# First layer's queries as seven half products per pair of heads, with keys and values of all heads computed first

## What is computed

```python
q = (query @ Wq).reshape(b, t, h, d)      # query = layernorm(x), b 16, t 64, h 32 heads, d 128
k = (key @ Wk).reshape(b, t, kv_h, d)     # key = value = context, 8 key/value heads
v = (value @ Wv).reshape(b, t, kv_h, d)
q = apply_rope(q)                         # x*cos + rotate_half(x)*sin
k = apply_rope(k)
logits = einsum('btkgd,bTkd->bkgtT', q, k) * ATTN_MULT
logits = 30 * tanh(logits / 30)
logits = where(mask, logits, -1e30)
attn = einsum('bkgtT,bTkd->btkgd', softmax(logits), v)
x = x + attn.reshape(b, t, h * d) @ Wo
```

## Time and profile before

| | before |
|---|---|
| median of 3 runs | 831.82 us (831.56 to 831.97) |
| profiled execution, its span | 830.6 us |
| TensorE busy | 825.8 us, 99% |
| VectorE busy | 549.1 us, 66% |
| ScalarE busy | 369.7 us, 45% |
| GpSimd busy | 361.4 us, 44% |
| granted TensorE clock | full speed in all 40 slices |

### The profile page before, as it was taken

The page is one execution under the profiler, slowest core; times in us unless marked ns, Lnnn a source line. Parts: engine busy times, 40 slices in busy tenths (PEclk is TensorE's granted clock), DMA queues, the critical chain, the costliest instruction groups (busy, mean ns, idle before and its releaser), DMA issues.

```text
span 830.6 us, 11973 instructions
## 1 busy us (share of the span) xinstructions
PE 825.8 (99%) x4382; PEld 687.4 (83%) x4382; DVE 549.1 (66%) x1091; ACT 369.7 (45%) x920; POOL 361.4 (44%) x279
## 2 busy tenths in 40 slices
PE   9999999999999999999999999999999999999998
PEld 7888888877887877877877788898988888888887
DVE  6866956767776564747767746464366657677894
ACT  6443223124213123122223142567797877777762
POOL 4777444545638324443645340112232432356442
PEclk9999999999999999999999999999999999999999
DMA  8122311311403202110311313011010210300002
GB/s 310 52 64 69 85 52 40 101 52 52 124 16 103 64 1 73 43 52 13 103 51 37 94 50 84 14 38 51 14 39 26 54 25 24 128 14 1 2 1 102
DMA packets 25786, 48.12 MB, mean 58 GB/s; under 512 B 4608, under 2 KB 5888, under 8 KB 25600
## 3 DMA queue, kind: packets, MB, share of 16 engines
q1 hardware_dynamic: 25296, 46.70, 19.0%
q10 hardware_dynamic: 432, 0.66, 0.2%
HBM read 45.12 MB, written 2.23 MB: 57 GB/s over the span
## 4 chain that ended last, share of the span: by engine, by line
PE 98%; DMA 1%; DVE 0%; ACT 0%; issue 0%; ACTq 0%; DVEq 0%
PE PB L1411 23%; PE PB L1412 23%; PE PB L1413 23%; PE PB L1627 8%; PE PB L1558 4%; PE PB L1541 4%; PE PB L1418 3%; PE PB L1642 3%; PE PB L1455 2%; PE PB L1453 2%; PE PB L1450 2%; DMA arena<-in_ctxT 1%; PE PB L1579 1%; PE PB L1593 0%; PE PB L1480 0%; PE PB L1473 0%
## 5 line engine op out<-in xcount | busy, mean ns | idle before, releaser
L912 POOL TENSOR_TENSOR qb<-qb,arena 128x512 f32<-128x512 f32 x64 | 83.8, 1310 | 151.1 <-DVE arena L1256 151.1
L1167 DVE TENSOR_TENSOR xs<-xs,PB 128x512 f32<-128x512 f32 x111 | 75.5, 686 | 79.0 <-PE PB L1413 70.0
L989 ACT ACTIVATE Oh<-PB 96x128 fp32r<-96x128 f32 (+2 forms) x236 | 79.4, 360 | 66.4 <-PE PB L1558 47.3
L1411 PE MATMUL PB<-WOh,Oh 128*128 128x512 f32 x242 | 94.5, 390 | 0.0
L1413 PE MATMUL PB<-WOh,Ol 128*128 128x512 f32 x242 | 94.2, 389 | 0.0
L1412 PE MATMUL PB<-WOl,Oh 128*128 128x512 f32 x242 | 94.2, 389 | 0.0
L989 ACT ACTIVATE WOh<-stage 128x512 fp32r<-128x512 f32 (+1 forms) x32 | 19.2, 620 | 132.6 <-PE PB L1413 132.6
L889 POOL TENSOR_TENSOR WOl<-stage,WOh 128x512 fp32r<-128x512 f32 (+1 forms) x32 | 40.7, 1284 | 83.5 <-ACT WOh L989 63.6
L889 POOL TENSOR_TENSOR WQl<-stage,WQh 128x512 fp32r<-128x512 f32 x38 | 49.0, 1293 | 61.7 <-ACT WQh L989 52.1
L1411 PE MATMUL PB<-xTh,WQh 128*128 128x512 f32 x188 | 74.8, 398 | 0.0
L1412 PE MATMUL PB<-xTl,WQh 128*128 128x512 f32 x188 | 73.3, 390 | 0.0
(11 more groups left out here) (294 smaller groups left out, 2171.2 us busy)
## 6 DMA issues: line engine op xcount, KB each, us to landing
stage<-in_wq SPq DMA_DIRECT2D x44, 256.0 KB, 2.7
stage<-in_wo SPq DMA_DIRECT2D x44, 256.0 KB, 2.7
arena<-recs SPq DMA_DIRECT2D x32, 256.0 KB, 3.9
stage<-in_wk SPq DMA_DIRECT2D x12, 256.0 KB, 2.6
xs<-in_x SPq DMA_DIRECT2D x8, 256.0 KB, 7.3
out<-xs SPq DMA_DIRECT2D x7, 256.0 KB, 2.0
arena<-in_ctxT SPq DMA_DIRECT2D x6, 256.0 KB, 7.0
stage<-in_wv SPq DMA_DIRECT2D x4, 256.0 KB, 4.8
```

The lines of the kernel that those rows point to most:

```text
L912: e.tensor_tensor(dst, dst, tmp, ALU.add).then_inc(s_radd)
L989: return e.activation(dst, src, ACT.Copy)
L1167: e.tensor_tensor(xs[:, i, :], xs[:, i, :], PB[b][:, :], ALU.add).then_inc(free[b])
L1411: e.matmul(dst, Ah, Bh, start=(k == 0), stop=False)
```

## The change

Per pair of query heads that belong to one key/value head (the pair is two of the group's four heads; u counts 14 pairs, of key/value heads 1 to 7) the four blocks of its queries (two heads, two halves of the tokens) are computed by Winograd's form of the product of two 2x2 block matrices: seven block products instead of eight, each of an inner dimension of 256 (two blocks of 128, so 6 matmuls). The factors of three of them are blocks as they are or two of them (products 1, 2, 3), of the others sums of blocks:

- x: the two halves of the tokens by the two halves of the inner dimension are the blocks. They are kept in f32 as `xf` when x is turned; four sums of them are formed once (`xt`, VectorE) and split to Th, Tl (`xt_split`: ScalarE, then VectorE or GpSimd), in the place of the context's parts.
- weights: `split wp u 0` and `wp u 1` split the two heads' weights into a buffer WS (1792 columns: head one whole, of head two the second block, then the four sums); GpSimd forms the four sums in `wsum` from the staged f32 weights (VectorE for u < 2), ScalarE writes their high part and GpSimd their low part (`pair`, 1024 columns each).
- products: 1, 6, 7, 4 accumulate one upon the other in one bank, 5 and 3 in a second, 2 alone in a third. ScalarE copies the bank after products 1, 5 and 6 into `held` (`snap`), VectorE adds products 2, 3 and 7 to these copies (`cmb`); the four finished tiles are the held ones and product 4's bank.
- rotations of these tiles (`rope p u t`, `sin u t`): ScalarE writes the two swapped, negated halves into a buffer rtmp, VectorE multiplies by cos into qb (a separate operation on the held tile, SBUF, for t < 3) and the buffer by sin in place (SBUF), GpSimd adds.

The queries of key/value head 0 (`q0`) stay as they were. Keys and values of all heads come first, in a stage before the loop: keys of heads 2 to 7 and values of heads 4 to 7 are written to DRAM (`keys`, `vals`; twenty spills of 256 KB on SyncE's queue out of eight slots in qb) and read back when a buffer comes free (`k_in`, `v_in`). The context's split parts go to DRAM (`ctx_out`, 4 MB in two DMAs) and come back at the end of the loop for layer 1 (`ctx_in`, issued by ScalarE). Homes of several split weights move, and `weff_load` is placed six turns earlier in layer 1's loop, behind a later wait.

In the loop's turn u a product pair stands for the four query steps, in pieces between the output tiles; the splits of the next pair's weights, `pair`, and in odd turns four splits of output weights are placed as the diff shows.

```diff
@@ plan @@
+    def more(self, *name, of):
+        bank, uses, _ = self.banks[of]
+        self.filled[bank] += 1
+        self.banks[name] = (bank, uses, self.filled[bank])
+        self.step(*name)
...
+    def products(u, *ks):
+        for k in ks:
+            if k in (6, 7, 4):
+                p.more("p", u, k, of=("p", u, 1))
+            elif k == 3:
+                p.more("p", u, k, of=("p", u, 5))
+            else:
+                stage("p", u, k, bank={1: 4 if u == 1 else 5, 2: 7, 5: 0}[k])
+            if k in (1, 5, 6):
+                step("snap", u, k)
+            elif k != 4:
+                step("cmb", u, k)
+
     for u in range(NU):
...
+        if u < 3:
+            products(u, 1, 2)
+            query(0)
+        burst(u)
+        if u % 2 and u <= 11:
+            step("k_in", (u + 3) // 2)
+        if u in (5, 9):
+            step("v_in", (u - 5) // 4)
+        query(3)
+        if u in (1, *range(3, NU)):
+            norm0(u - 1)
...
+        if quad:
+            if u >= 3:
+                products(u, 1, 2)
+            products(u, 5)
+            rope_p(u, 0)
+            sin(u, 0)
+        if u not in (1, 2):
+            step("sum0", u)
+            step("sum0_out", u)
+        outputs(0)
...
+        if quad:
+            products(u, 6, 3)
+            rope_p(u, 1)
+        if 0 < u < NU - 3:
+            for n in range(2):
+                split("wp", u + 1, n)
+        outputs(1)
+        if quad:
+            products(u, 7)
+            sin(u, 1)
+            query(2)
+            rope_p(u, 2)
+            sin(u, 2)
+        if u == 2:
+            norm0(1)
+        if u in (1, 2):
+            step("sum0", u)
+            step("sum0_out", u)
+        outputs(2)
+        if quad:
+            products(u, 4)
+            rope_p(u, 3)
+            sin(u, 3)
+        if 0 < u < NU - 3:
+            step("pair", u + 1)
+        outputs(3)
+        if u % 2:
+            for n in range(4):
+                split("wo0", 2 * u - 2 + n)
@@ gpsimd_program @@
+                            e.tensor_tensor(parts[0], other[:, 0:256], other[:, 256:512], ALU.add).then_inc(s_ws)
+                            e.tensor_tensor(parts[2], src[:, 0:256], other[:, 0:256], ALU.subtract).then_inc(s_ws)
+                            pool.wait_ge(s_ws, 4 * u + 1)
+                            e.tensor_tensor(parts[1], parts[0], src[:, 0:256], ALU.subtract).then_inc(s_ws)
+                            pool.wait_ge(s_ws, 4 * u + 3)
+                            e.tensor_tensor(parts[3], src[:, 256:512], parts[1], ALU.subtract).then_inc(s_ws)
...
+                elif kind == "pair" and k[0] >= 2:
+                    u, = k
+                    hi, lo = WS[1 - u % 2]
+                    pool.wait_ge(s_wshi, u + 1)
+                    e.tensor_tensor(lo[:, 768:1792], wsum[:, :], hi[:, 768:1792].bitcast(f32), ALU.subtract).then_inc(s_wslo)
@@ scalar_program @@
+                elif kind == "snap":
+                    u, t = k
+                    act.wait_ge(*done("p", u, t))
+                    if u:
+                        act.wait_ge(s_sin, 4 * u - {1: 3, 6: 2, 5: 1}[t])
+                    move(held[t], PB[bank_of("p", u, t)][:, :]).then_inc(s_snap)
+                elif kind == "rope" and k[0] == "p":
...
+                    act.wait_ge(s_radd, n - 2)
+                    for r in range(2):
+                        last = e.activation(tmp_of(n)[64 * r:64 * r + 64], src[64 - 64 * r:128 - 64 * r], ACT.Copy, scale=-1.0)
+                    last.then_inc(s_swap)
@@ vector_program @@
+                elif kind == "rope" and k[0] == "p":
...
+                    cos = e.tensor_tensor(dst, src.rearrange("p (b t) -> p b t", b=8), ropeq[:, 0:1, :].broadcast_to([128, 8, 64]), ALU.mult)
...
+                elif kind == "sin":
...
+                    e.tensor_tensor(tmp, tmp, ropeq[:, 1:2, :].broadcast_to([128, 8, 64]), ALU.mult).then_inc(s_sin)
+                elif kind == "cmb":
...
+                    e.tensor_tensor(kept, PB[bank_of("p", u, t)][:, :], kept, ALU.add).then_inc(s_cmb)
@@ tensor_program @@
+                    pe.wait_ge(*(lo_ready("wp", u, t // 4) if t in (1, 2, 4) else (s_wslo, u + 1)))
...
+                    fresh = t in (1, 2, 5)
+                    for c in range(2):
+                        w = slice(c0 + 128 * c, c0 + 128 * c + 128)
+                        for n, (W, X) in enumerate(((Wh, Xh), (Wh, Xl), (Wl, Xh))):
+                            last = e.matmul(PB[b][:, :], W[:, w], X[:, c, :], start=fresh and c == n == 0, stop=(c == 1 and n == 2),
+                                            skip_group_check=not fresh)
+                    last.then_inc(full[b])
```

534 lines of the change are left out of this document (412 added, 122 removed).

## The result

| | before | after |
|---|---|---|
| median of 4 runs | 831.69 us | 885.79 us (885.31 to 886.53) |
| profiled execution, its span | 830.6 us | 883.8 us |
| TensorE busy | 99% | 94% |
| two units in the middle of the loop | 57.0 us (scores at 198.70 and 255.72), TensorE full, products of later keys and values among them | 55.6 us, of which TensorE's work needs 48.4 |

The ratio is 1.0646, 95% interval 1.0631 to 1.0661: 54.1 us slower. The forecast was 858 us, range 824 to 872; the direction was right, the size half of what was measured.

A forecast was written before the change was run, and what follows sets the result against it. The prediction took TensorE, busy 99% of the span and holding 98% of the chain, to bound the kernel. From 831.8 us, -19.0 (products), +32 (loop) and +13 (opening) gave 858 us, range 824 to 872.

The forecast's parts named there:

- The products saved: TensorE's query products: 84 fewer at 0.226 us each, -19.0 us.
- The new first stage: Keys and values of all heads ahead of the queries: same products, 0 to +4 us, taken as 0.
- The loop: Units 2 to 13: waits through the other engines' queues outlast TensorE's work; 7 to 35 us, taken as +32.
- The eleven steps: Loop from one unit's mask to the next without TensorE: 21.8 us, 22.4 with handoffs; 55 for two units with turns.
- step 5: In the loop, ScalarE's high part of the next pair's weights, behind its swap for the second rotation: 0.6 us.
- the port's turns: VectorE operations with two SBUF inputs alternate with GpSimd's: up to 0.55 us each; two units 55 us against 51.5.
- B: Rival: the loop without most turns and an opening of 8; 836 us, 829 to 843, chance 0.19.
- C: Rival: a loop link seen wrongly, two units take TensorE's 48.4, opening costs 5; 818 us, 813 to 824, chance 0.17.
- The opening: Units 0 and 1, without output products as cover: TensorE waits 5 to 16 us, taken as +13.
- The end: Units 14 and 15, context read back for layer 1, moved weight homes: 0, within +-2 us.
- Rival D: TensorE idles several us at a stretch and its clock falls; 20 us more, about 880, chance 0.07.
- A: The forecast case: the queue loop with port turns decides; 844 to 870, around 858 us, chance 0.57.

The follow-up runs named there:

- e2: d1 with the parts of the weight sums placed behind product 7's rotation; 837.13 us.
- b1: The changed kernel with the splits of the next pair's weights ahead of the row sums instead of behind product 3's rotation; 851.11 us.
- d1: b1 and b4 joined, with the round trip of unit 1's row sums behind the four splits of output weights; 840.06 us.
- b4: The changed kernel with both halves of the context's parts read back at the start of turn 14, ahead of layer 1 weight splits; 876.77 us.
- e1: d1 without the two sine operations on VectorE in each of the eight rotations of key/value head 0's queries; 833.97 us.
- b8: The changed kernel with 10, 12 and 12 unused products ahead of three TensorE waits in the opening; 886.46 us.
- b2: The changed kernel with its sine products multiplying by a constant instead of the sine table; 872.14 us.
- c6: c5 with ScalarE swapping the halves for key/value head 0's queries and VectorE multiplying twice instead of three times; 855.39 us.
- c5: b1 and b4 joined, pair 2's weights split at the end of turn 0, and pair 1's weight sums formed by GpSimd instead of VectorE; 846.36 us.

## Why the prediction was wrong in size

**The products saved** (-19.0): right. e2's turns of 24.4 us are the 24.2 that were worked out for a full TensorE.

**The new first stage** (0, up to +4): about right. TensorE is busy 96.70 of the first 100 us where it was 97.89.

**The loop** (+32): right in mechanism and size, +35.7. The eleven steps gave 55 us for two units and the trace 55.6; b1 shows that step 5 held it, and the rows of GpSimd's sums (4.08 us for 3.09), though no edit by itself, say that the port's turns are a part of the price. Rivals B (no turns) and C (a link wrong) fell.

**The opening** (+13, 5 to 16): this step failed; it is +26.0 and 2.45 ahead of it. The step took turn 0 (up to 6; measured 24.6 - 19.5 = 5.1 and the 2.45) and the stretch from unit 1's scores to the last output weight (9), by the chain of GpSimd and ScalarE alone. That chain was sized about right: 26 us were forecast, and the last output weights are ready at 175.20, 27.7 us after the end of unit 1's scores (147.5). But TensorE did not wait for them.

```profile
174.53 0.79 PE L1827 MATMUL PB<-Th,WSh 128*128 128x512 f32 x1 [3.10 <-DVE Ol L1675]
...
177.26 0.63 PE L1790 MATMUL PB<-WVh,Oh 128*128 128x512 f32 x1
...
197.90 1.76 PE L1969 MATMUL PB<-pTb,arena 64*128 64x256 f32 x6 [2.39 <-DVE xs L1476]
...
172.69 2.51 POOL L1139 TENSOR_TENSOR W<-stage,W 128x512 fp32r<-128x512 f32 x2
```

It came to the first output product only at 177.26, 29.8 us after that end for 14.7 of work: 15.1 lost where the step said 9. Ahead of it lie three waits of TensorE that the step did not have: for VectorE's addition (3.02), for the low part of pair 2's weights (3.12) and for VectorE's low part of the outputs (3.10), with half clock from 157.57 on. The last of them came through SyncE's queue: the load of an output weight stood there behind a wait for VectorE's row sums, and ScalarE's copies behind that load. The prediction itself names the queues past which a moved step is carried; this one was not followed. d1, which moves it, is 2.0 us below the sum of b1 and b4. The rest of turn 2 lost another 4.2, with a wait of 2.39 for an output tile's addition, and turn 3 1.5; the step stopped short of both. What would remove the 14.5 us that are left in e1 stays open.

**The end** (0, within 2): wrong, +9.0. The prediction counted work on engines and the queues' loads, and not what 4 MB on the DMA engines does to an 8 KB round trip on which VectorE waits.

**Rival D** (half clock, +20 on top, 0.07): the clock did fall, in the opening and near 546 us. It was set up as an alternative to A where both came at once; and its price was wrong where it was tested, since TensorE would have waited anyway (b8; and d1, with a clock of 0.92 or more in each turn, still has an opening of 99.1 us).

**The range** ended at 872 because the bounds of the opening (16) and of the end (2) were bounds of what had been counted. With the measured 28.4 and 9.0 in their places the same sum is -19 + 32 + 28.4 + 9.0 = +50.4.

## What to carry to other kernels

Engines of which none is over 67% busy can still bind together: follow one loop through the queues in their order, with durations from rows, as was done here for two units; it gave 55 for 55.6, and the one step to move (b1) gave back 35 of 54 us. Follow the first turns and the last ones with the same care as the steady ones, with the DMA queues as links of the chain, since there is the least cover. Where the engine waits for others, half clock can be a symptom, as in b8: price the wait first.

## What the runs showed that was not expected

- An 8 KB transfer took 6.4 us to land beside two of 1 MB, where it takes 1.7 in the loop, and two of 256 KB behind it, beside two more of 1 MB, 8.4 for 3.9.
- Filling three waits of TensorE with 34 products kept the clock full in those stretches (1.00 for 0.61 at 155 to 165 us) and changed the time by less than 1 us; the clock fell behind a later wait instead.
- A product of 512 columns by a constant in SBUF took VectorE 0.42 us by itself and up to 1.51 beside GpSimd (b2): one SBUF input did not keep it out of the turns.
- Replacing three VectorE operations that read PSUM by two, of which one reads SBUF behind a ScalarE move, cost 9 us (c6 against c5).
